# A graph network's tile loop: three stretches of first-layer units a tile instead of two, and two-tile groups at the end

## The chip, the cores and the metric

One core of one Trainium2 chip. The metric is the device time of one launch in microseconds; the time before is the median of three runs.

## The reference, cut to what matters

```python
# 6250 nodes, 200000 edges sorted by destination, 200 edge types, D = 128
# layer 0: attention over the edges of each node
e = leaky_relu(a_src[src] + a_dst[dst] + a_rel[etype], 0.01)
w = exp(e - segment_max(e, dst)[dst])
agg = segment_sum(w / segment_sum(w, dst)[dst] * x[src], dst)
x = layernorm(x + where(deg > 0, agg, x) + x @ loop_weight)
# then two layers of this, h = x at first:
msg = (rel_embed[etype] + h[src]) @ W_r
h = rrelu(segment_sum(msg, dst) * deg ** -0.5 + where(deg == 0, h @ W_el, h @ W_sl))
# and out = layernorm(x + h)
```

## The kernel before, in words

The nodes are cut into 50 tiles of 125. The kernel has three parts: a loop over the tiles (attention and everything that the two later layers need), the rest of the first message layer, and the second message layer.

**The tile loop.** For tile t, POOL gathers the rows of the tile's edges (33 indirect transfers, L605, issued a tile ahead into one of two buffers). VectorE adds the score terms (L1227, the first step of `weights`), works out the softmax's maxima in two exchanges with TensorE (L921 and L928), and ScalarE turns the result into 33 weighted one-hot matrices, which TensorE multiplies with the gathered rows (L938). Meanwhile VectorE prepares tile t+1: the wide comparisons on L1170, and in `prepare_edges` (L1197 on) two large tables of one-hots, one for the nodes, one for the 200 edge types; both are made on L1193, as are the smaller ones of the batches. TensorE multiplies the two tables in `types_in` (L836).

**The counts.** A tile's adjacency with all 50 source tiles is a matrix of counts, built in seven batches (`batch`: VectorE makes one-hots on L1193, TensorE multiplies them on L859, ScalarE copies them out, each batch needing the copy of the second one before). SyncE stores the matrix in HBM; `at_stored` counts the stores.

**Units and stretches.** The message of the first layer into a group of destination tiles is a sum over 52 units: two for the edge types and one for each of the 50 source tiles. A unit can be computed when the source tile has left the loop (`hs_ready`) and the counts of the whole group are stored. It is three matmuls (L872) with one column for each destination node of the group: 500 for a group of four tiles, 250 for the last one, of two. There are 12 groups of four and one of two.

A table made when the program is built (L84 to L94) gives each tile, from tile 6 on, up to two stretches: at most 12 consecutive units of one group each, the group with the most units ready first. A stretch (`stretch`) is loaded in pieces of four units into `held`, which has two places: a piece can be loaded (L518, `load_held`, on SyncE's queue) when the piece two before it is done (`held_done`). A stretch accumulates in PSUM bank 6, and VectorE adds it to the group's sum (`stretch_sum`, L1306) before the next stretch may begin (`st_read`).

The order on each engine is written out by hand. On TensorE, for a tile between the first and the last: the small products for the maxima; stretch 0, piece 0; the accumulation L938; `terms`; stretch 0, piece 1; batch 0; stretch 0, piece 2; batches 1 and 2; `types_in` of the next tile; batch 3; `types`; stretch 1, piece 0; batches 4 to 6; `x1_in` (a transposition); stretch 1, piece 1; `x1_node` (the node product, L898); stretch 1, piece 2. On VectorE: `weights`, `prepare_wide`, batches 0 and 1, `prepare_edges`, the sum of stretch 0, batch 2, `finalize`, batch 3, `normalise`, batches 4 to 6, `terms`; the sum of stretch 1 stands at the head of the next tile's `weights`, ahead of L1227. On SyncE: the lists of tile t+2, the loads of pieces 1 and 2 of stretch 0, the wide lists, `reshape_terms` (L491 to L496: a store of the score terms, a wait for it, and a load), the loads of stretch 1, and then `store_counts`.

**The rest of the first layer.** What the stretches left over (148 units) is loaded through a ring (`load_piece`) and multiplied group by group. VectorE finishes a group in two steps (`finish`, L1393 and L1396), and then each of its tiles gets a node product (L994, `node_m`), which ScalarE and VectorE turn into the second layer's weights; TensorE puts a group's node products between the units of the next. **The second layer** (L1037, L1039) runs over the 50 destination tiles.

## Time and profile before

| | |
|---|---|
| median of three runs | 2718.59 us (2717.42 to 2721.06) |
| the profiled execution | 2715.95 us, span 2714.0 us |
| TensorE busy | 2153.3 us, 79% of the span |
| VectorE busy | 1971.8 us, 73% |
| POOL busy | 1584.6 us, 58% |
| ScalarE busy | 1219.5 us, 45% |
| tile loop | up to 2157 us |
| rest of the first layer | 2157 to 2282 us |
| second layer | 2282 us to the end |

The profile comes from one execution. PE is TensorE, PEld its weight loads, DVE is VectorE, ACT ScalarE, POOL GpSimd, SP SyncE. In brackets stands how long the engine stood idle just before an instruction, and what ended that.

### The profile page before, as it was taken

Reading aid. Unit: us, or ns where it says so; the run is one execution under the profiler, and the core shown is the slowest. Engines: PE = TensorE matmul, PEld = TensorE weight load, DVE = VectorE, ACT = ScalarE, POOL = GpSimd, SP = SyncE. Lnnn points to the kernel's source line nnn. Section 1 sums busy time; section 2 is a strip of 40 time slices with the busy share of each in tenths; the row PEclk is TensorE's granted clock in tenths of the full one; section 3 lists DMA queues with packets and bytes.
Section 4 is the critical chain, followed back from the end, with each engine's and each line's share of the span. In section 5 each row is a group of like instructions: output and inputs, shape, how many; then the busy total and the mean of one; then the engine's idle time right before and its main releaser. Section 6 shows DMA issues by size and latency. Waiting matters only on the chain. (4 is left out here: it accounts for less than half of the span.)

```text
span 2714.0 us, 44262 instructions
## 1 busy us (share of the span) xinstructions
PE 2153.3 (79%) x15636; PEld 1612.5 (59%) x15636; DVE 1971.8 (73%) x4330; ACT 1219.5 (45%) x3215; POOL 1584.6 (58%) x1672
## 2 busy tenths in 40 slices
PE   1466676767677787786887878888888889999998
PEld 0355565655555555655565656556656536888887
DVE  6788888888888888878888888888778562333333
ACT  1265565565555555554555555655545441000000
POOL 6767777777777777777777777777777000000000
PEclk9888888888888888898988989989999999999999
DMA  8545555656555565655666667667666435666664
GB/s 226 173 127 158 174 157 161 195 156 190 173 184 174 177 193 166 210 181 180 215 186 198 217 183 217 200 198 234 197 211 209 144 108 186 213 213 212 214 214 154
DMA packets 265971, 507.43 MB, mean 187 GB/s; under 512 B 106240, under 2 KB 203832, under 8 KB 245921
## 3 DMA queue, kind: packets, MB, share of 16 engines
q1 hardware_dynamic: 197394, 383.10, 43.3%
q0 software_dynamic: 53600, 114.17, 16.3%
q10 hardware_dynamic: 14752, 7.26, 1.0%
q8 instruction: 128, 2.10, 0.3%
q14 instruction: 97, 0.79, 0.1%
HBM read 406.54 MB, written 97.84 MB: 186 GB/s over the span
## 5 line engine op out<-in xcount | busy, mean ns | idle before, releaser
L605 POOL DMA_INDIRECT arena<-rows,srcw x1617 | 1535.0, 949 | 510.4 <-issue 490.7
L1193 DVE TENSOR_TENSOR arena<-bank,idx 128x2000 bf16<-128x2000 bf16 (+3 forms) x700 | 562.1, 854 | 93.6 <-PE pair L859 87.8
L859 PE MATMUL pair<-arena 128*128 128x250 bf16 x2500 | 344.5, 286 | 283.1 <-DVE arena L1193 273.2
L627 ACT ACTIVATE arena<-pair 99x264 f32<-99x264 f32 (+2 forms) x410 | 282.3, 713 | 556.3 <-PE pair L859 420.1
L729 ACT ACTIVATE arena<-arena,wexp 128x125 f32<-128x125 bf16 x1650 | 483.3, 385 | 1.6
L872 PE MATMUL bank<-arena 125*128 125x500 bf16 (+1 forms) x1950 | 465.2, 387 | 12.2 <-DMA arena<-counts 11.7
L859 PEld LDWEIGHTS pair<-arena 128*128 128x128 bf16 x2500 | 243.5, 102 | 372.5 <-DVE arena L1193 308.3
L938 PE MATMUL bank<-arena 128*125 128x130 f32 x3300 | 448.8, 295 | 0.0
L938 PEld LDWEIGHTS bank<-arena 128*125 128x125 f32 x3300 | 417.2, 201 | 24.3
L1039 PE MATMUL pair<-arena 125*125 125x384 bf16 x2500 | 414.8, 326 | 0.0
L1039 PEld LDWEIGHTS pair<-arena 125*125 125x125 bf16 x2500 | 341.0, 136 | 66.1 <-issue 0.4
L1170 DVE TENSOR_TENSOR arena<-arena,bank 128x4224 bf16<-128x4224 int16 x150 | 344.2, 2350 | 1.7
L872 PEld LDWEIGHTS bank<-arena 125*128 125x128 bf16 x1950 | 189.0, 100 | 229.7 <-issue 67.4
L836 PE MATMUL pair<-arena 128*125 128x200 bf16 x1650 | 210.5, 305 | 10.1 <-DVE arena L1193 10.1
L836 PEld LDWEIGHTS pair<-arena 128*125 128x125 bf16 x1650 | 209.2, 181 | 12.9 <-issue 10.9
L1411 DVE SCALAR_TENSOR_TENSOR arena<-pair,norm,arena 125x128 f32<-125x128 f32 x50 | 17.5, 351 | 272.1 <-PE pair L1039 272.1
L776 ACT ACTIVATE rstd<-mv,epst 125x1 f32<-125x1 f32 x50 | 14.7, 294 | 407.5 <-DVEq L1433 407.5
L1193 DVE TENSOR_TENSOR arena<-bank,et 128x6600 bf16<-128x6600 bf16 x50 | 179.2, 3584 | 0.0
L661 ACT ACTIVATE arena<-pair 128x500 bf16<-128x500 f32 x150 | 95.8, 639 | 108.7 <-PE pair L859 105.3
L1193 DVE TENSOR_TENSOR arena<-bank,dl 128x4224 bf16<-128x4224 bf16 x50 | 117.9, 2358 | 1.7
L1306 DVE TENSOR_TENSOR arena<-bank,arena 128x500 f32<-128x500 f32 x80 | 54.4, 679 | 47.8 <-PE bank L872 44.9
L826 PE MATMUL pair<-arena,Zd 125*3 125x264 bf16 x800 | 62.0, 278 | 29.8 <-DVE arena L1170 17.7
(243 smaller groups left out, 2009.6 us busy)
## 6 DMA issues: line engine op xcount, KB each, us to landing
arena<-counts SPq DMA_DIRECT2D x104, 812.5 KB, 4.5
counts<-arena SPq DMA_DIRECT2D x50, 1562.5 KB
arena<-counts SPq DMA_DIRECT2D x112, 500.0 KB, 3.8
arena<-dst SPq DMA_DIRECT2D x50, 1056.0 KB
arena<-etype SPq DMA_DIRECT2D x50, 1056.0 KB
arena<-rows,srcw POOLq DMA_INDIRECT x1617
arena<-counts SPq DMA_DIRECT2D x11, 750.0 KB, 4.4
arena<-counts SPq DMA_DIRECT2D x23, 250.0 KB, 4.1
```

Source lines behind the costliest of these rows:

```text
L605: pool.indirect_dma_start(out=rows[:, q, c, :], out_offset=None, in_=rows0, in_offset=bass.IndirectOffsetOnAxis(ap=srcw[:, q, c:c + 1], ax ...
L627: act.activation(o, i, ACT.Copy).then_inc(s("ev"), 1)
L661: act.activation(AT[:, :, d0:d0 + 2 * G], two, ACT.Copy)
L729: r = act.activation(hot[:, c % HOTS, :], hotb[:, c, 0:TN], ACT.Copy, scale=wexp[:, c:c + 1])
L826: pe.matmul(o, Zd[0:TN, t % 2, 0:3], hotT[0:TN, cs], start=True, stop=False)
L836: r = pe.matmul(b_[0:TN, 0:R], hotb[:, c, 0:TN], toh[:, c, :], start=(c == 0), stop=(c == C - 1))
L859: r = pe.matmul(group_of(n, gi), ohl[:, sl, gi * GC + c, :], ohm[:, sl, gi * GC + c, :], start=(c == 0), stop=(c == GC - 1))
L872: r = pe.matmul(o, w, moving[0:n_], start=start and j == 0, stop=stop and j == 2)
L938: r = pe.matmul(sums[0:TN, 0:D + 2], hot[:, c % HOTS, :], rows[:, q, c, 0:D + 2], start=(c == 0), stop=(c == C - 1))
L1039: r = pe.matmul(o, part[0:TN, u - u0, :], hs1[0:TN, u - 2, :], start=False, stop=(u == HS - 1))
L1170: return v.tensor_tensor(out_.rearrange("p (j t) -> p j t", t=2), list_.rearrange("p (j t) -> p j t", t=2), two[:, None, :].broadcast_to(s ...
L1193: return v.tensor_tensor(hot_.rearrange("p c (j t) -> p c j t", t=2), iotap[:, 0:w].rearrange("p (j t) -> p j t", t=2)[:, None, :, :].broa ...
```

## The change

It does five things. The thirteen groups become fourteen: eleven of four tiles and three of two (`GSIZES`); a piece of a two-tile group holds eight units. From tile 30 on a tile has a third stretch, of at most 8 units of a four-tile group, and its pieces, like those of stretch 1, stand between the batches. The second stretch may take a group as soon as its last tile is a tile behind, the first one a tile later as before. On VectorE, `prepare_edges` is cut in two, and batch 2 stands between the halves; the sum of stretch 0 stands behind the second. On TensorE the first two units of stretch 0 are issued apart: one ahead of the products for the maxima, one between the two exchanges.

```diff
@@ -76,34 +76,42 @@
...
 GT = 4
-NGR = -(-NT // GT)
+GSIZES = (4,) * 11 + (2,) * 3
+GAT = [sum(GSIZES[:g_]) for g_ in range(len(GSIZES) + 1)]
+NGR = len(GSIZES)
+GROUP_OF = [g_ for g_ in range(NGR) for _ in range(GSIZES[g_])]
 HOTS = 26
 NU = 4
-SLEN = 3 * NU
+THIRD = 30
+SLENS = (3 * NU, 3 * NU, 2 * NU)
 STRETCH, DONE_U = {}, [0] * NGR
 for t_ in range(6, NT):
-    for k_ in range(2):
+    for k_ in range(3 if t_ >= THIRD else 2):
         best = None
         for g_ in range(NGR - 1):
-            n_ = min(SLEN, t_ + 1 + k_ - DONE_U[g_])
-            if GT * g_ + GT + 1 <= t_ and n_ >= 2 and STRETCH.get((t_, 0), (NGR,))[0] != g_ and (best is None or n_ > best[0]):
+            w_ = GSIZES[g_]
+            n_ = min(SLENS[k_] * GT // w_, t_ + (1, 1 if t_ >= THIRD else 2, 2)[k_] - DONE_U[g_])
+            if GAT[g_ + 1] + (k_ == 0) <= t_ and n_ * w_ >= 2 * GT and STRETCH.get((t_, k_ - 1), (NGR,))[0] != g_ \
+                    and (best is None or n_ * w_ > best[0] * GSIZES[best[1]]):
                 best = (n_, g_)
-        if best is not None:
-            n_, g_ = best
-            STRETCH[t_, k_] = (g_, DONE_U[g_], DONE_U[g_] + n_)
-            DONE_U[g_] += n_
+        if best is None:
+            break
+        n_, g_ = best
+        STRETCH[t_, k_] = (g_, DONE_U[g_], DONE_U[g_] + n_)
+        DONE_U[g_] += n_
 STRETCHES = list(STRETCH)
...
     g_, u_, e_ = STRETCH[key_]
-    for i_ in range(-(-(e_ - u_) // NU)):
+    nu_ = NU * GT // GSIZES[g_]
+    for i_ in range(-(-(e_ - u_) // nu_)):
         HELD_AT[key_ + (i_,)] = len(HELD)
-        HELD.append((key_, g_, u_ + i_ * NU, min(u_ + i_ * NU + NU, e_)))
+        HELD.append((key_, g_, u_ + i_ * nu_, min(u_ + i_ * nu_ + nu_, e_)))
     HELD_TO[key_] = len(HELD)
...
 def tiles_of(g):
-    return range(GT * g, min(GT * g + GT, NT))
+    return range(GAT[g], GAT[g + 1])
 
...
@@ -514,9 +522,10 @@
...
                     sp.wait_ge(s("held_done"), n - 1)
-                sp.wait_ge(s("at_stored"), 32 * GT * (g + 1))
-                sp.dma_start(held[:, n % 2, 0:GT * (u1 - u0) * TN].rearrange("p (t f) -> p t f", t=GT),
-                             counts[GT * g:GT * g + GT, :, u0 * TN:u1 * TN].rearrange("t p f -> p t f")).then_inc(s("held%d" % (n % 2)), 16)
+                w = GSIZES[g]
+                sp.wait_ge(s("at_stored"), 32 * GAT[g + 1])
+                sp.dma_start(held[:, n % 2, 0:w * (u1 - u0) * TN].rearrange("p (t f) -> p t f", t=w),
+                             counts[GAT[g]:GAT[g + 1], :, u0 * TN:u1 * TN].rearrange("t p f -> p t f")).then_inc(s("held%d" % (n % 2)), 16)
 
...
@@ -560,6 +569,8 @@
...
                 load_held(t, 1, 2)
+                load_held(t, 2, 0)
+                load_held(t, 2, 1)
                 load_held(t + 1, 0, 0)
...
@@ -872,21 +883,24 @@
...
 
-            def stretch(t, k, i):
+            def stretch(t, k, i, a=0, b=None):
                 if (t, k, i) not in HELD_AT:
...
                 m = STRETCHES.index(key)
-                if i == 0 and m >= 1:
+                v0, v1 = min(u0 + a, u1), u1 if b is None else min(u0 + b, u1)
+                if i == 0 and a == 0 and m >= 1:
                     pe.wait_ge(s("st_read"), m)
...
                 pe.wait_ge(s("held%d" % (n % 2)), 16 * (n // 2 + 1))
-                part = held[:, n % 2, 0:GT * (u1 - u0) * TN].rearrange("p (t u d) -> p t u d", t=GT, d=TN)
-                for u in range(u0, u1):
-                    r = unit(per_tile(bank[6][:, 0:GT * TN], GT), part[:, :, u - u0, :], u, u == STRETCH[key][1], u == STRETCH[key][2] - 1)
-                r.then_inc(s("held_done"), 1)
+                w = GSIZES[g]
+                part = held[:, n % 2, 0:w * (u1 - u0) * TN].rearrange("p (t u d) -> p t u d", t=w, d=TN)
+                for u in range(v0, v1):
+                    r = unit(per_tile(bank[6][:, 0:w * TN], w), part[:, :, u - u0, :], u, u == STRETCH[key][1], u == STRETCH[key][2] - 1)
+                if v0 < v1 == u1:
+                    r.then_inc(s("held_done"), 1)
 
...
@@ -917,6 +931,7 @@
...
                     self_in(t + 1)
+                stretch(t, 0, 0, 0, 1)
                 pe.wait_ge(s("th_ready"), t + 1)
...
@@ -924,10 +939,11 @@
...
                     own_turned(t - 1)
+                stretch(t, 0, 0, 1, 2)
                 pe.wait_ge(s("cf_ready"), t + 1)
...
                 pe.matmul(bank[0][:, 2 * P + 1:2 * P + 2], cfb[0:1, 1, :], ones[0:1, 0:1], start=True, stop=True).then_inc(s("cf_ps"), 1)
-                stretch(t, 0, 0)
+                stretch(t, 0, 0, 2)
                 if t >= 1:
...
@@ -977,21 +993,33 @@
...
                     stretch(t, 1, 0)
-                    for j in range(4, BT):
-                        batch(t, j)
+                    batch(t, 4)
+                    if (t, 2) in STRETCH:
+                        stretch(t, 1, 1)
+                    batch(t, 5)
+                    if (t, 2) in STRETCH:
+                        stretch(t, 1, 2)
+                    batch(t, 6)
                     x1_in(t)
-                    stretch(t, 1, 1)
+                    if (t, 2) in STRETCH:
+                        stretch(t, 2, 0)
+                    else:
+                        stretch(t, 1, 1)
                     x1_node(t)
-                    stretch(t, 1, 2)
+                    if (t, 2) in STRETCH:
+                        stretch(t, 2, 1)
+                    else:
+                        stretch(t, 1, 2)
 
...
@@ -1195,6 +1223,10 @@
...
             def prepare_edges(t):
+                edge_nodes(t)
+                edge_types(t)
+
+            def edge_nodes(t):
                 q = t % 2
...
@@ -1205,6 +1237,8 @@
...
                 paired(hotb, dl2, C)
+
+            def edge_types(t):
                 paired(toh, et2, C).then_inc(s("hot_ready"), 1)
...
@@ -1218,7 +1252,7 @@
...
                 if t >= 1:
-                    stretch_sum(t - 1, 1)
+                    stretch_sum(t - 1, 2 if (t - 1, 2) in STRETCH else 1)
                 v.wait_ge(s("dr_summed"), t + 1)
...
@@ -1370,17 +1405,20 @@
...
                         batch(t, j)
-                    if more:
-                        prepare_edges(t + 1)
+                    edge_nodes(t + 1)
+                    batch(t, 2)
+                    edge_types(t + 1)
                     stretch_sum(t, 0)
-                    batch(t, 2)
                     finalize(t)
...
                         batch(t, j)
+                    if (t, 2) in STRETCH:
+                        stretch_sum(t, 1)
                 if more:
                     terms(t + 1)
+            stretch_sum(NT - 1, 2)
             v.wait_ge(s("st_read"), len(STRETCHES))
```

What is left out replaces `GT * g` by `GAT[g]` and `GT` by the group's own width in `stretch_sum`, `finish` and `node_m`.

## Rows read from the trace of the kernel before

**Rows 1.** The page: a group of part 5, and an issue of part 6.

```profile
L605 POOL DMA_INDIRECT arena<-rows,srcw x1617 | 1535.0, 949 | 510.4 <-issue 490.7
...
arena<-counts SPq DMA_DIRECT2D x112, 500.0 KB, 3.8
```

**Rows 2.** Stretches of time: PE, PEld, DVE, ACT, POOL busy; PEclk, DMA share, GB/s.

```profile
1330.00:2120.00 790.00, 671.04 (x5066) 473.11 (x5066) 659.69 (x1367) 437.95 (x1144) 589.93 (x624) 0.93 0.66 202
...
2157.00:2240.00 83.00, 71.75 (x282) 33.95 (x281) 47.69 (x149) 36.19 (x132) 0.00 (x0) 1.00 0.38 116
```

**Rows 3.** Timeline, L1227 on DVE in tiles 26, 30, 49; the last gather on POOL.

```profile
1161.67 0.21 DVE L1227 TENSOR_TENSOR u<-arena,dr 128x33 f32<-128x33 f32 x1 [2.80 <-DMA arena<-rows,srcw]
...
1329.24 0.20 DVE L1227 TENSOR_TENSOR u<-arena,dr 128x33 f32<-128x33 f32 x1
...
2108.86 0.94 POOL L605 DMA_INDIRECT arena<-rows,srcw  x1 [0.30 <-issue]
...
2119.65 0.20 DVE L1227 TENSOR_TENSOR u<-arena,dr 128x33 f32<-128x33 f32 x1
```

**Rows 4.** Timeline of DVE in tile 46, 1992.5 to 2035 us.

```profile
1992.59 0.20 DVE L1227 TENSOR_TENSOR u<-arena,dr 128x33 f32<-128x33 f32 x1
...
2012.94 3.59 DVE L1193 TENSOR_TENSOR arena<-bank,et 128x6600 bf16<-128x6600 bf16 x1
...
2017.56 1.79 DVE L1193 TENSOR_TENSOR arena<-bank,idx 128x2000 bf16<-128x2000 bf16 x2
...
2021.23 1.79 DVE L1193 TENSOR_TENSOR arena<-bank,idx 128x2000 bf16<-128x2000 bf16 x2
...
2028.76 1.41 DVE L1193 TENSOR_TENSOR arena<-bank,idx 128x1500 bf16<-128x1500 bf16 x2 [2.33 <-PE pair L859]
...
2033.75 0.68 DVE L1306 TENSOR_TENSOR arena<-bank,arena 128x500 f32<-128x500 f32 x1 [3.25 <-PE bank L872]
...
2034.35 0.20 DVE L1227 TENSOR_TENSOR u<-arena,dr 128x33 f32<-128x33 f32 x1
```

**Rows 5.** Timeline of PE in tile 46, 1998 to 2036 us.

```profile
2019.40 1.04 PE L859 MATMUL pair<-arena 128*128 128x250 bf16 x8 [2.41 <-DVE arena L1193]
...
2020.28 2.99 PE L836 MATMUL pair<-arena 128*125 128x200 bf16 x33
...
2025.36 2.71 PE L872 MATMUL bank<-arena 125*128 125x500 bf16 x12 [1.11 <-DMA arena<-counts]
...
2030.23 0.82 PE L859 MATMUL pair<-arena 128*128 128x250 bf16 x6 [0.85 <-DVE arena L1193]
...
2035.12 0.38 PE L921 MATMUL bank<-ident,lf 128*1 128x128 f32 x2 [0.66 <-DVE lm_in L1230]
```

**Rows 6.** Timeline of SP in tile 46, 2004 to 2030 us.

```profile
2020.69 0.39 SPq L496 DMA_DIRECT2D drw<-edge_terms  x1
...
2021.18 0.98 SPq L518 DMA_DIRECT2D arena<-counts  x2
```

**Rows 7.** Timeline of PE in tile 34, 1519 to 1529 us.

```profile
1521.63 1.04 PE L859 MATMUL pair<-arena 128*128 128x250 bf16 x8 [2.47 <-DVE arena L1193]
...
1522.51 4.65 PE L836 MATMUL pair<-arena 128*125 128x200 bf16 x33
```

**Rows 8.** Timeline of DVE, L1396 of groups 0, 10, 11 and 12.

```profile
2160.38 0.68 DVE L1396 SCALAR_TENSOR_TENSOR arena<-arena 128x500 f32<-128x500 f32 x1
...
2234.53 0.68 DVE L1396 SCALAR_TENSOR_TENSOR arena<-arena 128x500 f32<-128x500 f32 x1
...
2262.59 0.68 DVE L1396 SCALAR_TENSOR_TENSOR arena<-arena 128x500 f32<-128x500 f32 x1
...
2282.55 0.42 DVE L1396 SCALAR_TENSOR_TENSOR arena<-arena 128x250 f32<-128x250 f32 x1
```

**Rows 9.** Timeline of PE after the loop, 2239 to 2284 us.

```profile
2240.53 21.31 PE L872 MATMUL bank<-arena 125*128 125x500 bf16 x99
...
2267.00 15.06 PE L872 MATMUL bank<-arena 125*128 125x250 bf16 x138
```

18 lines of the change are left out of this document (10 added, 8 removed).

## The prediction

> **What bounds the kernel now.** I read the grouped lines first, to find an engine that never rests in the tile loop. It is POOL: 1617 gathers of 0.949 us with 490.7 us of issue gaps between them and next to no waiting [rows 1]. One gather costs 1.25 us, so the 33 of a tile take 41.2 us, and no tile can be quicker than that. The stretches of time come next [rows 2]: between 1330 and 2120 us (tiles 30 to 48) TensorE is busy for 671 of 790 us and VectorE for 660, neither of them full. From 2157 us the loop is over and the rest of the first layer runs, and from 2282 us the second layer, which TensorE fills and the change does not touch.
>
> Then I followed one instruction through the tiles, the addition on L1227 that opens a tile's softmax; I call its time u. At 1161.67 us (tile 26) it still waits 2.80 us for the gather, so up to there POOL sets the pace. At 1329.24 (tile 30) and 2119.65 (tile 49) it waits for no gather any more, and the last gather was issued at 2108.86 [rows 3]. So 19 tiles took 790.4 us, 41.6 each, where POOL alone asks for 41.2, and at the end the loop is some 9 us behind the gathers. **From tile 30 on it is not POOL but the exchange between VectorE and TensorE that decides, by a small margin.** That is the place where the change adds work.
>
> Inside tile 46 (u = 1992.59, next u = 2034.35, period 41.76) VectorE has the nodes' table behind it and starts the types' table on L1193 at u+20.4, then the one-hots of batch 2 at u+25.0 and of batch 3 at u+28.6, ready at u+30.4 [rows 4]. TensorE waits 2.41 us ahead of batch 2, runs the types table in 2.99 us, and starts the first piece of the second stretch at u+32.8, after 1.11 us of waiting for its load [rows 5]. That load was issued only at u+28.6, because SyncE stood at the reshaped terms, whose last transfer it issues at u+28.1 [rows 6]. From u+32.8 everything on TensorE stands in the way of the next tile: 8 units of a stretch, three batches, a transposition. The sum on L1306 waits 3.25 us for the last unit, and the next u follows it at once [rows 4]. **A unit put ahead of batch 3 is free as long as it fills the hole; a unit put behind it is paid in full.**
>
> **The change, step by step.** One unit of a four-tile group is three matmuls of 500 columns; 99 of them take 21.31 us, 0.215 each, 0.644 us a unit. 138 matmuls of 250 columns take 15.06 us, 0.109 each [rows 9]. A unit of a two-tile group is thus 0.327 us and costs per tile what the wide one does. Below, n counts four-tile units and two narrow ones are one.
>
> (1) The tail after the loop. The plan leaves 148 units before (56 in groups 0 to 10, 40 in group 11, 52 narrow ones in group 12) and 105 after (45 in groups 0 to 10, 8 narrow ones in groups 11 and 12, 52 narrow ones in group 13). Groups 0 to 10 finish on L1396 from 2160.38 to 2234.53, ten steps of 7.4 us [rows 8], while TensorE is busy for 71.75 of 83 us [rows 2]: node products and units, partly overlapped. Eleven units fewer are worth between 0 and 7 us; I take 3. Group 11 then finishes at 2262.59 and group 12 at 2282.55, 28.1 and 20.0 us further [rows 8]. In their place come two short groups, each between half a step and a whole one (3.7 to 7.4; I take 5, as each has two nodes but the whole handshake), and the last group with two interleaved node products fewer, 18.7 us: 28.7 in place of 48.0. The tail gains 19.3 + 3 = **22 us, between 17 and 26**.
>
> (2) The loop takes on what the tail gives up: 188 tile-units, 47 n, or 30 us of TensorE. But it also moves units. Which, the file's own planning loop tells (the one that the diff rewrites), worked through for both versions. In tiles 30 to 48 the first stretch, which lies ahead of batch 3, falls from 199 n to 134. The second and third, which lie behind it, rise from 121 to 220, since a new group now enters the second stretch as soon as it is complete (12 n in tiles 32, 36, 40, 44, 46 and 48) and the third adds 3 to 8 n in each tile. So 99 n move into the part that is paid.
>
> (3) Price of a tile. Before: 32.8 us to the first piece of stretch 1, 0.644 n, and 3.85 us for batches 4 to 6, the transposition and the sum (tile 46: 32.8 + 5.15 + 3.85 = 41.8). Summed over 19 tiles with 121 n this is 774 us against the 790.4 measured. The 16 us between are mostly clock: in tile 34 the types table takes 4.65 us, where it takes 2.99 in tile 46, after the same wait of 2.4 us [rows 7, 5], and the granted clock of the stretch is 0.93 [rows 2]. After: the wait of 0.85 us ahead of batch 6 [rows 5] is filled in tiles whose second stretch has more than one piece, and one node product (0.65 us) moves ahead of the last piece where the third has two; I leave 3.85. With the table again at 32.8, for the queue that sets the load is the same, 19 x 36.65 + 220 x 0.644 = 838 us, **48 us more than before**. Ends: if the first piece starts at u+31.6, the end of batch 3 and the small products without the load's wait, 23 us less, so +25; if the clock stays as it is, 16 more, and if each tile with a second piece in the third stretch waits for held loads, 9 more, so +73.
>
> (4) Batch 2 between the tables. VectorE does the same work in another order: batch 2 is ready near u+22.5 but the types table only near u+26.2, and batch 3 where it was, near u+31 (half a microsecond later, as batch 2 now waits for batch 0's products). TensorE's hole of 2.41 us is cut into one of about 1 ahead of the table and one of 1.7 behind it. Gain: nothing by itself, since batch 3 is what counts; if the table falls into the slow clock again it no longer delays batch 3, and that is why (3) takes the full clock.
>
> (5) The first piece's units spread. They fill the waits of 0.66 us for L921 [rows 5] and the like one behind it. The accumulation that follows waits for ScalarE's weights, so I cost this at nothing (0 to 0.2 us a tile, 4 in all). It adds a risk: L921, with the whole softmax chain behind it, now stands behind a held load. Such a load takes 3.8 us to land [rows 1] and can be issued only when the piece two before it is done; where the third stretch ends in a piece of one or two units that is 1 to 2 us late. This is the 9 us in (3).
>
> (6) 19 more sums on L1306 at 0.68 us [rows 4] are 13 us of VectorE; it waits 5.6 us in a tile for TensorE, so they hide, and one more is in the period of a tile only through its wait. SyncE's two more loads a tile stand ahead of the counts' store, which waits for the next tile's weights anyway.
>
> Tiles 6 to 29 also change (58 to 111 n behind batch 3), but there POOL has the pace and VectorE waits for the gathers, 2.80 us in tile 26 [rows 3]; that wait takes up the 1.4 us a tile that 53 n make, and is their only cover (without it they cost 34 us); I add 1 us for tile 30 starting later and nothing for tile 49.
>
> Sum: 48 + 1 - 22 = +27. The profiled execution took 2715.95 us (span 2714.0), the median of the runs is 2718.6, 2.6 us above. I forecast **2744 us** as a median: 2716 + 27 is 2743, and I round the 2.6 against the part of (5) that may gain. A difference within 0.2%, 5.4 us, can't be told from none.
>
> One rule of the Trainium skill speaks against the narrow groups. The rows say 0.109 us for 250 columns and 0.215 for 500, so no loss [rows 9]. TensorE: Matmul & The Clock Gate, section Back-to-back issue gap, gives for streams of weight load and matmul 81 ns at 128 columns and 131 at 512; an estimate from that page, 97 ns at 250 and 130 at 500, would make each of the 288 narrow matmuls in the loop 32 ns dearer than its half of a wide one, 9 us more. The trace does not agree, and the sum leaves it out.
>
> **The rivals.** A, faster: the third stretch falls into holes. If the loop keeps within POOL's pace, u of tile 49 can't come before the last gather has landed, about 2112 us, up to 8 us earlier than now, and the tail's 22 us come on top: 2718.6 - 22 and down to -30, so **2694**. For it speaks that TensorE stands idle for 119 of the 790 us [rows 2] and only 30 us are added; against it that these holes lie ahead of batch 3, where the plan takes units away. It decides if the third piece's start is below about u+30 in most tiles.
>
> B, the cost only cancels the gain: the first piece starts at u+31.6 and half the light tiles hide their third stretch, +22 in the loop: **2718**, no difference.
>
> C, slower still: the clock. The row shows half speed for the table after a wait of 2.4 us, in most tiles. If the two smaller holes pull it down as the one did, now in front of 12 units that are paid, the 16 us stay and the late loads of (5) come on top: **2768**. The same page's section on the clock gate says that the array falls to 1.2 GHz after idleness and comes back with sustained work; by that rule the denser tail of a tile should run at 2.4 GHz, which is my main case, and rows 7 agree with its first half.
>
> **How the numbers follow.** Main case 0.50 (own range 2724 to 2762), A 0.25, B 0.10, C 0.15. Faster 0.25, same 0.10, slower 0.65. The range takes half of A and most of C: 2695 to 2768.
>
> **What would show it.** In the profile after: L1227 from tile 30 to 49 some 838 us apart instead of 790; periods near 41 in tiles with 7 n behind batch 3 and near 47 in tiles 44, 46 and 48; no wait for gathers there; the last wait of L1306 or of L872 for a load in those tiles; L836 at 2.99 us or no longer followed by a late batch 3; group 13's finish about 103 us behind the loop's end in place of 125. I am wrong if the 19 tiles take under 800 us, which would mean that units behind batch 3 are not paid, or if the tail gains under 15.

## The result, and the profile after

The changed kernel takes **2781.05 us** (median, 2777.82 to 2784.44), the kernel before 2719.82 us beside it on the same chip (2717.42 to 2723.16): a ratio of 1.0225, interval 1.0212 to 1.0238. So it is slower by 61 us, where 27 were forecast; 2781 lies above the range, whose upper end was 2768. The profiled execution has a span of 2781.4 us against 2714.0, 67.4 us more. In twelve of the runs below the kernel before itself took 4448 to 4451 us, with stretches of some 20 us in which no engine works, so these runs stand apart at the end and nothing is read from them.

The page of the changed kernel, its costliest groups and the DMA issues. L616 is L605 of before, L883 is L872, L847 is L836, L870 is L859:

```profile
L616 POOL DMA_INDIRECT arena<-rows,srcw x1617 | 1536.5, 950 | 566.6 <-issue 487.4
...
L883 PE MATMUL bank<-arena 125*128 125x500 bf16 (+1 forms) x2100 | 456.1, 360 | 41.8 <-DMA arena<-counts 36.1
...
L847 PE MATMUL pair<-arena 128*125 128x200 bf16 x1650 | 230.7, 323 | 117.1 <-DVE arena L1221 107.6
...
arena<-counts SPq DMA_DIRECT2D x118, 500.0 KB, 5.2
```

Against [rows 1] a gather costs the same, but POOL now rests for 56 us more, and a held load of 500 KB lands after 5.2 us, not 3.8. TensorE waits 36.1 us for held loads.

The timeline of VectorE in the changed kernel, the addition that opens a tile (L1261, L1227 of before) in tiles 16, 17, 30 and 49, and POOL's last gather:

```profile
752.39 0.21 DVE L1261 TENSOR_TENSOR u<-arena,dr 128x33 f32<-128x33 f32 x1 [5.63 <-DMA arena<-rows,srcw]
801.10 0.20 DVE L1261 TENSOR_TENSOR u<-arena,dr 128x33 f32<-128x33 f32 x1
1349.48 0.20 DVE L1261 TENSOR_TENSOR u<-arena,dr 128x33 f32<-128x33 f32 x1
2204.75 0.20 DVE L1261 TENSOR_TENSOR u<-arena,dr 128x33 f32<-128x33 f32 x1
...
2168.07 0.95 POOL L616 DMA_INDIRECT arena<-rows,srcw  x1 [0.30 <-issue]
```

Against [rows 3]: tile 30 opens 20.2 us later, tile 49 85.1 us later, so tiles 30 to 48 took 855.3 us in place of 790.4. The finishes after the loop, L1434 (L1396 of before), of groups 0, 10, 11, 12 and 13:

```profile
2251.04 0.68 DVE L1434 SCALAR_TENSOR_TENSOR arena<-arena 128x500 f32<-128x500 f32 x1
...
2321.20 0.68 DVE L1434 SCALAR_TENSOR_TENSOR arena<-arena 128x500 f32<-128x500 f32 x1
...
2327.31 0.42 DVE L1434 SCALAR_TENSOR_TENSOR arena<-arena 128x250 f32<-128x250 f32 x1
...
2331.60 0.42 DVE L1434 SCALAR_TENSOR_TENSOR arena<-arena 128x250 f32<-128x250 f32 x1
...
2350.01 0.42 DVE L1434 SCALAR_TENSOR_TENSOR arena<-arena 128x250 f32<-128x250 f32 x1
```

Ten steps take 70.2 us (before 74.2), the last groups 6.1 + 4.3 + 18.4 = 28.8 us (before 28.1 + 20.0) [rows 8]. From u of tile 49 to the first finish it is 46.3 us, where it was 40.7.

**The four stretches add up.** Tiles 0 to 29 lose 20.2 us, tiles 30 to 48 lose 64.9, tile 49 loses 5.6, the tail gains 23.3: 67.4, the whole difference of the spans. The forecast had +1, +48, 0 and -22.

Inside a late tile, TensorE in tile 44 of the changed kernel (u = 1962.52, period 49.84, 17 n behind batch 3):

```profile
1964.48 0.80 PE L883 MATMUL bank<-arena 125*128 125x500 bf16 x3 [2.49 <-DMA arena<-counts]
...
1965.21 0.38 PE L936 MATMUL bank<-ident,lf 128*1 128x128 f32 x2
...
1970.35 0.19 PE L860 MATMUL bank<-onesb,arena 128*125 128x1 bf16 x1 [1.23 <-issue]
...
1990.20 4.65 PE L847 MATMUL pair<-arena 128*125 128x200 bf16 x33 [1.84 <-DVE arena L1221]
...
1997.72 1.44 PE L883 MATMUL bank<-arena,relW 128*128 128x500 bf16 x6 [1.68 <-DMA arena<-counts]
```

and VectorE there (L1269 reads the transposed row, L1341 is the sum of a stretch):

```profile
1965.84 0.41 DVE L1269 TENSOR_TENSOR_SCAN XY<-full,bank 1x128 f32<-1x128 f32 x1 [2.06 <-PE bank L937]
...
2006.98 0.68 DVE L1341 TENSOR_TENSOR arena<-bank,arena 128x500 f32<-128x500 f32 x1 [4.44 <-PE bank L883]
2011.76 0.68 DVE L1341 TENSOR_TENSOR arena<-bank,arena 128x500 f32<-128x500 f32 x1 [3.78 <-PE bank L883]
```

The first unit, spread ahead of the transposition L936, waits 2.49 us for its load, and VectorE waits 2.06 us for the transposition behind it. In tile 46 of before nothing stood there but 0.66 us for VectorE [rows 5]. The stretch sums wait 8.2 us in the tile, the last with the next u right behind it: units behind batch 3 are paid.

SyncE's queue in tiles 43 and 44 of the changed kernel (L527 issues the held loads; the first row is the last reshaped term, after which they go out):

```profile
1947.53 0.39 SPq L504 DMA_DIRECT2D drw<-edge_terms  x1
1948.01 0.43 SPq L527 DMA_DIRECT2D arena<-counts  x1
1950.77 0.27 SPq L516 DMA_DIRECT2D dense_input<-arena  x1
1951.14 9.85 SPq L527 DMA_DIRECT2D arena<-counts  x3
1970.32 0.34 SPq L510 DMA_DIRECT2D counts<-arena  x1
```

Three held loads go out one by one from 1951.1 to 1961.0, each as TensorE gives a buffer back; the last is the next tile's first piece. It leaves 1.5 us ahead of u and lands 3.5 us later.

Grouped lines of TensorE by form, 1350 to 2205 us, tiles 30 to 48 of the changed kernel (busy, mean ns | idle before, by what):

```profile
L883 PE MATMUL bank<-arena 125*128 125x500 bf16 x930 | 220.7, 378 | 19.5 <-DMA arena<-counts 16.6 <-DVE arena L1341 2.7
...
L847 PE MATMUL pair<-arena 128*125 128x200 bf16 x627 | 84.7, 316 | 38.4 <-DVE arena L1221 31.3 <-ACT arena L638 7.1
...
L883 PE MATMUL bank<-arena 125*128 125x250 bf16 x204 | 26.0, 285 | 1.7 <-DMA arena<-counts 1.7
...
L944 PE MATMUL bank<-ones,cfb 1*128 1x1 f32 x38 | 7.4, 261 | 2.9 <-DVE cfb L1272 2.9
...
L860 PE MATMUL bank<-onesb,arena 128*125 128x1 bf16 x19 | 3.6, 192 | 25.2 <-issue 22.3 <-ACT arena L740 2.8
...
L883 PE MATMUL bank<-arena,relW 128*128 128x500 bf16 x12 | 3.2, 374 | 5.6 <-DMA arena<-counts 5.6
```

And the same of the kernel before, 1330 to 2120 us:

```profile
L872 PE MATMUL bank<-arena 125*128 125x500 bf16 x936 | 228.5, 393 | 3.2 <-DMA arena<-counts 3.2
...
L836 PE MATMUL pair<-arena 128*125 128x200 bf16 x627 | 80.9, 307 | 0.0
...
L928 PE MATMUL bank<-ones,cfb 1*128 1x1 f32 x38 | 7.2, 256 | 16.9 <-DVE cfb L1238 16.9
```

TensorE lost 14 us of waiting at L928's place, but got 22.3 us ahead of L860, the accumulation that needs ScalarE's weights, and the wait for held loads rose from 3.2 us to 22 in the two rows of wide units alone (16.6 and 5.6). The types table did not get quicker: 84.7 us of TensorE for 19 tables, where 80.9 were before.

**Where a late tile got longer.** Every period can be cut in three, as step (3) of the prediction does: the start of the second stretch's first piece on TensorE, counted from u; 0.644 us a unit; and the rest. In tiles 30 to 48 the forecast had 32.8 us for the start and 3.85 for the rest. The timeline has, in the mean, 33.66 and 3.84 before, and 33.47 and 4.09 in the changed kernel: 12.7 and 4.6 us above the forecast over 19 tiles.

### The profile page after: what moved, and what is told of

It reads as the page before. It is cut to its first block and busy times, and to the rows that moved or that the text cites. A ratio compares the mean times of both kernels' runs of the same rounds, so it can differ in the third digit from the quotient of the medians.

```text
span 2781.4 us, 44709 instructions
## 1 busy us (share of the span) xinstructions
PE 2182.9 (78%) x15792; PEld 1653.5 (59%) x15792; DVE 1978.5 (71%) x4351; ACT 1219.8 (44%) x3215; POOL 1587.3 (57%) x1672
## 5 line engine op out<-in xcount | busy, mean ns | idle before, releaser
L616 POOL DMA_INDIRECT arena<-rows,srcw x1617 | 1536.5, 950 | 566.6 <-issue 487.4
L883 PE MATMUL bank<-arena 125*128 125x500 bf16 (+1 forms) x2100 | 456.1, 360 | 41.8 <-DMA arena<-counts 36.1
L954 PE MATMUL bank<-arena 128*125 128x130 f32 x3300 | 483.3, 308 | 0.0
L954 PEld LDWEIGHTS bank<-arena 128*125 128x125 f32 x3300 | 447.4, 212 | 28.4
L870 PE MATMUL pair<-arena 128*128 128x250 bf16 x2500 | 322.7, 275 | 158.2 <-DVE arena L1221 142.5
L870 PEld LDWEIGHTS pair<-arena 128*128 128x128 bf16 x2500 | 235.6, 99 | 240.8 <-DVE arena L1221 186.0
L883 PEld LDWEIGHTS bank<-arena 125*128 125x128 bf16 x2100 | 198.0, 98 | 232.6 <-issue 66.3
L847 PE MATMUL pair<-arena 128*125 128x200 bf16 x1650 | 230.7, 323 | 117.1 <-DVE arena L1221 107.6
L847 PEld LDWEIGHTS pair<-arena 128*125 128x125 bf16 x1650 | 221.5, 192 | 130.7 <-issue 108.4
L1341 DVE TENSOR_TENSOR arena<-bank,arena 128x500 f32<-128x500 f32 (+1 forms) x99 | 66.1, 668 | 141.1 <-PE bank L883 139.8
```

The costliest lines, as they stand in the source:

```text
L616: pool.indirect_dma_start(out=rows[:, q, c, :], out_offset=None, in_=rows0, in_offset=bass.IndirectOffsetOnAxis(ap=srcw[:, q, c:c + 1], ax ...
L847: r = pe.matmul(b_[0:TN, 0:R], hotb[:, c, 0:TN], toh[:, c, :], start=(c == 0), stop=(c == C - 1))
L870: r = pe.matmul(group_of(n, gi), ohl[:, sl, gi * GC + c, :], ohm[:, sl, gi * GC + c, :], start=(c == 0), stop=(c == GC - 1))
L883: r = pe.matmul(o, w, moving[0:n_], start=start and j == 0, stop=stop and j == 2)
L954: r = pe.matmul(sums[0:TN, 0:D + 2], hot[:, c % HOTS, :], rows[:, q, c, 0:D + 2], start=(c == 0), stop=(c == C - 1))
L1341: v.tensor_tensor(a, per_tile(bank[6][:, 0:w * TN], w), a, ALU.add).then_inc(s("st_read"), 1)
```

## The experiments

The disputed parts are four: the third stretch, the rule by which a new group enters the plan, the spread first piece, and batch 2 between the tables. The six runs beside a kernel before of 2719 to 2722 us come first. The other twelve stand at the end of this section with what they were expected to show.

**Run a4c: the old entry rule.** The third stretch stays, but a new group waits one tile, as before.

```diff
-            if GAT[g_ + 1] + (k_ == 0) <= t_ and n_ * w_ >= 2 * GT and ...
+            if GAT[g_ + 1] + 1 <= t_ and n_ * w_ >= 2 * GT and ...
```

> Once more, alone on its chip: the changed kernel with the old rule for when a group may enter a stretch, so that a new group's first 12 units go to the first stretch: 54 instead of 111 four-tile units behind batch 3 in tiles 6 to 29, 188 instead of 220 in tiles 30 to 48. If the place of a unit decides: the 20 us of delay at tile 30 go, and 20 more behind it: 2741. If only the number of units counts, no difference: 2781.

Measured: 2750.04 us, ratio 1.0108 (1.0091 to 1.0125), 31 us less than the changed kernel and 9 above what was expected. Its tiles 30 and 49 on VectorE:

```profile
1329.59 0.21 DVE L1261 TENSOR_TENSOR u<-arena,dr 128x33 f32<-128x33 f32 x1 [2.87 <-DMA arena<-rows,srcw]
...
2162.68 0.20 DVE L1261 TENSOR_TENSOR u<-arena,dr 128x33 f32<-128x33 f32 x1
```

The delay up to tile 30 is gone, to 0.3 us, and u waits for the gather again. The rule is what cost the 20 us there, and another 22 us in tiles 30 to 48 (833.1 us with 188 n behind batch 3, against 855.3 with 220). The run does not tell the burst from the amount: it has 54 n behind batch 3 in tiles 6 to 29 instead of 111, and puts them in no tile more than 4.

**Run a1c: the first piece whole.** The changed kernel, but all units of the first piece behind the second exchange, as before.

```diff
-                stretch(t, 0, 0, 0, 1)
...
-                stretch(t, 0, 0, 1, 2)
...
-                stretch(t, 0, 0, 2)
+                stretch(t, 0, 0)
```

> Once more, alone on its chip: the changed kernel with the first piece of stretch 0 whole again, behind the second exchange for the maxima. If a unit ahead of L936 makes the softmax chain wait for its held load (1.3 to 2.6 us in tiles 33, 43, 44, 45, 47, 48 and 49 of the changed kernel's trace, 14 us in all), 2767 us. If the spread units only fill holes, no difference: 2781. If they gained a hole's 0.65 us in the other tiles, 2790.

Measured: 2758.6 us, ratio 1.0148 (1.0131 to 1.0165), 22 us less than the changed kernel and 8 below what was expected of it. Grouped lines of TensorE by form, 1339 to 2183 us (L935 and L943 are L936 and L944 of the changed kernel):

```profile
L883 PE MATMUL bank<-arena 125*128 125x500 bf16 x930 | 228.0, 395 | 7.9 <-DMA arena<-counts 7.5
...
L935 PE MATMUL bank<-ident,lf 128*1 128x128 f32 x38 | 7.2, 271 | 17.9 <-DVE lm_in L1262 17.9
...
L860 PE MATMUL bank<-onesb,arena 128*125 128x1 bf16 x19 | 3.5, 184 | 1.8 <-issue 1.8
```

The load's wait falls by 9.1 us in the wide units (16.6 to 7.5) and the 22.3 us ahead of L860 are gone, while TensorE waits 17.9 us for the first exchange. So the spread had only moved TensorE's wait from the exchange to the weights, and put a load on the path of the softmax. Tiles 30 to 48 took 844.4 us (1338.63 to 2182.98), 10.9 less, and 10.8 came off before tile 30. The 10.9 lie where the first unit had waited for its load: tiles 33, 43, 44, 45, 47 and 48 are 11.3 us shorter together, the other thirteen 0.4 longer. The first piece of the second stretch now starts at u+32.87 in the mean, 0.60 earlier, and no unit waits ahead of the first exchange any more.

**Run d1b: no third stretch, old entry rule.** Groups of two, the tables' order and the spread stay.

```diff
-THIRD = 30
+THIRD = NT
...
-            if GAT[g_ + 1] + (k_ == 0) <= t_ and n_ * w_ >= 2 * GT and ...
+            if GAT[g_ + 1] + 1 <= t_ and n_ * w_ >= 2 * GT and ...
```

> Again, since the kernel before took 4448 us on the chip of the last run: the changed kernel without the third stretch and with the old entry rule; two-tile groups, spread first piece and the tables' order kept. Against the kernel with the old rule (2750) it has 128 four-tile units behind batch 3 in tiles 30 to 48 instead of 188, and 33 more left for the tail: 39 us less in the loop by 0.64 us a unit, no late first pieces, 10 to 20 us more in the tail: 2700 to 2715. If the third stretch filled holes, 2760 to 2770. If the tail's gain from two-tile groups is what my sum said, it ends below the kernel before.

Measured: 2720.28 us, ratio 1.0008 (0.9998 to 1.0018): no difference from before, and 5 us above what was expected. Against a4c this prices the third stretch: 60 n fewer behind batch 3, tiles 30 to 48 in 800.8 us in place of 833.1 (0.54 us a unit), and 30 us by the medians. The 0.54 is too low as the price of a unit, for these tiles had become quick enough to meet the gathers again: u waits 12.8 us for them in tiles 31 to 41. Its finishes of groups 10 to 13:

```profile
2251.94 0.68 DVE L1434 SCALAR_TENSOR_TENSOR arena<-arena 128x500 f32<-128x500 f32 x1
...
2258.06 0.42 DVE L1434 SCALAR_TENSOR_TENSOR arena<-arena 128x250 f32<-128x250 f32 x1
...
2268.69 0.42 DVE L1434 SCALAR_TENSOR_TENSOR arena<-arena 128x250 f32<-128x250 f32 x1
...
2287.09 0.42 DVE L1434 SCALAR_TENSOR_TENSOR arena<-arena 128x250 f32<-128x250 f32 x1
```

Groups 11 to 13 take 35.2 us instead of 48 for the last two of before, but the ten steps ahead of them 81.1 (from 2170.87) instead of 74.2. The plan leaves 72 wide units in groups 0 to 10 and 32 narrow ones in groups 11 and 12, where before left 56 and 40 wide ones in group 11. What the small groups gain in the tail is mostly spent on the older ones.

**Run e1: the same with the first piece whole.** The edits of a1c and d1b together.

> The changed kernel without its third stretch, with the entry rule of before and with the first piece whole again behind the second exchange; groups of two tiles and the tables' order stay. The kernel with these but with a spread first piece took 2720.3 us (before 2719.0). Theory: the spread costs in every tile in which GpSimd's list does not set the pace, because a held load that lands late then stops TensorE ahead of the exchanges: 22 us were found beside the third stretch (11 of them by tile 30); here only tiles 42 to 48 are free of GpSimd's pace, 7 tiles by 0.6 to 1.2 us: 2713 to 2717 us, tile 48 and 47 long as before (48.6 and 44.6 us). Rival: the spread costs only beside a third stretch or beside twelve units of a new group behind batch 3: 2720, no change. Rival: it pays where it stands alone: 2722 to 2725.

Measured: 2717.33 us, ratio 0.9993 (0.9984 to 1.0002), against 1.0008 with the spread. Tiles 30 to 48 took 796.1 us (1332.10 to 2128.21), 4.7 less than in d1b, of which 3.5 in tile 47 (45.2 us, was 48.6), which was expected to stay. The time is at the upper end of what the theory gave, and the two intervals overlap by a little, so I call it likely, not shown, that the spread costs some 3 us even alone. It is the best version found, and can't be told from the kernel before.

**Run b2b: batch 2 between the tables, alone**, in the kernel before.

```diff
-                    if more:
-                        prepare_edges(t + 1)
-                    stretch_sum(t, 0)
-                    batch(t, 2)
+                    edge_nodes(t + 1)
+                    batch(t, 2)
+                    edge_types(t + 1)
+                    stretch_sum(t, 0)
```

> The kernel before with batch 2 alone moved between the next tile's node tables and its type tables; groups, two stretches and the whole first piece stay. Theory (from the changed kernel's first five tiles, which took 36.5 to 37.5 us in place of 38.6 to 40.1): about 1.9 us a tile are saved where GpSimd's list does not set the pace: tiles 1 to 5 (then taken back by GpSimd's pace up to tile 41), and tiles 42 to 48; 2705 to 2715 us. Rival: the table order gains nothing anywhere but in tiles 1 to 5, where nothing stands behind batch 3: 2718 to 2721. Rival: batch 3's start moves later with the stretch sum and the order costs a little: 2722 to 2728.

Measured: 2719.47 us, ratio 0.9998 (0.9988 to 1.0007). The rival holds: no gain. Grouped lines of TensorE, 1330 to 2126 us:

```profile
L872 PE MATMUL bank<-arena 125*128 125x500 bf16 x936 | 236.4, 403 | 12.7 <-DMA arena<-counts 12.7
L859 PE MATMUL pair<-arena 128*128 128x250 bf16 x950 | 119.5, 271 | 48.8 <-DVE arena L1193 48.6
L836 PE MATMUL pair<-arena 128*125 128x200 bf16 x627 | 66.2, 271 | 29.5 <-ACT arena L627 16.7 <-DVE arena L1193 12.8
```

The order does for the types table what I expected: 66.2 us for 19 tables in place of 80.9, 14 of them at 3.02 us, where before only two ran at 2.99. The table now starts behind a wait of its own (29.5 us in all) and the units wait 12.7 us for loads, where they waited 3.2. Still the first piece of the second stretch starts at u+33.02 in the mean, where it was u+33.66: 12.0 us earlier over the 19 tiles. And yet these tiles took 795.6 us (1330.04 to 2125.67), 5.2 more than before. The trace shows two things that took the gain.

The first is POOL's pace. Tiles 31 to 36 now open with 9.0 us of waiting for gathers, tile 31 most of all, where before no tile behind 26 did:

```profile
1371.39 0.21 DVE L1233 TENSOR_TENSOR u<-arena,dr 128x33 f32<-128x33 f32 x1 [3.27 <-DMA arena<-rows,srcw]
```

The second is the clock. It left the table and fell on units that are paid: the first 12 matmuls of the second stretch take 5.16, 4.24, 4.24 and 4.38 us in tiles 37, 38, 41 and 46, with a granted clock of 0.50 to 0.61 over them, and 2.71 us before. Tile 37 of b2b, TensorE and the stretch of time (columns as in [rows 2], the granted clock is 0.50), and the same piece before:

```profile
1650.61 1.04 PE L859 MATMUL pair<-arena 128*128 128x250 bf16 x8 [1.80 <-DVE arena L1193]
...
1652.78 5.16 PE L872 MATMUL bank<-arena 125*128 125x500 bf16 x12 [1.02 <-DMA arena<-counts]
```

```profile
1652.70:1658.00 5.30, 5.22 (x14) 1.98 (x15) 1.13 (x2) 0.33 (x3) 4.07 (x5) 0.50 0.30 70
```

```profile
1650.61 2.71 PE L872 MATMUL bank<-arena 125*128 125x500 bf16 x12
```

Before, these matmuls took 0.23 or 0.24 us each in all 19 tiles. The four tiles are 7.6 us longer behind the piece's start. So of the 12.0 us gained, 9.0 went into waits for gathers and 7.6 into the lower clock: 4.6 more than was gained, of the 5.2 us lost. This is one execution, 3.8 us above b2b's median; how often the clock falls on these pieces is not known. That the earlier start is worth nothing is therefore not shown: the kernel before had only some 8 us to gain here before it met the gathers (19 times 41.2 us is 783, against 790.4). Tiles 1 to 5, which have no stretches, did get 1.6 us shorter in the mean (37.4 to 37.8 us, where they took 38.6 to 40.1), and POOL's pace took that back.

**Run c2b: another way to use the hole ahead of batch 3.** Groups of two with the old rule, the old order and a whole first piece, plus a fourth piece of the first stretch ahead of batch 2, and the second stretch's first load issued a step earlier. The sum of stretch 0 moves behind batch 3. The edit on TensorE:

```diff
-SLENS = (3 * NU, 3 * NU, 2 * NU)
+SLENS = (4 * NU, 3 * NU, 2 * NU)
...
-                    for j in range(1, 3):
-                        batch(t, j)
+                    batch(t, 1)
+                    stretch(t, 0, 3)
+                    batch(t, 2)
```

> The kernel with two-tile groups alone, a fourth piece of the first stretch ahead of batch 2, and the load of the second stretch's first piece issued ahead of SyncE's wait for the stored terms, once more: in the eight runs above the kernel before took 4432 to 4457 us, with stretches of 20 us in which no engine worked, so their differences say nothing of this case. If the kernel before takes 2720 again: 2675 to 2685 where units ahead of batch 3 are free and the load holds the second stretch; 2690 where only the first holds; 2705 to 2715 where a unit is paid wherever it stands. If the kernel before takes 4450 again, the 20 us stretches belong to the chip of these runs.

Measured: 2778.4 us, ratio 1.0217 (1.02 to 1.0234), a clear miss. The fourth piece on TensorE in tile 30 (u = 1336.22), and SyncE's queue there (L494 loads two wide lists of 1056 KB each, L499 stores the terms, L530 is a held load):

```profile
1368.82 3.91 PE L888 MATMUL bank<-arena 125*128 125x500 bf16 x9 [6.38 <-DMA arena<-counts]
```

```profile
1355.69 0.36 SPq L494 DMA_DIRECT2D arena<-dst  x1
1356.15 0.38 SPq L494 DMA_DIRECT2D arena<-etype  x1
1356.58 1.44 SPq L499 DMA_DIRECT2D edge_terms<-arena  x4
1358.18 3.81 SPq L530 DMA_DIRECT2D arena<-counts  x2
```

The load was issued at 1358.2 and TensorE could go on at 1368.8: 10.6 us for a held load behind 2.1 MB on the same queue, where such a load lands in 3.8 [rows 1]. In tiles 30 to 48 TensorE waits 60.7 us for held loads, where it waited 3.2 before. A tile with a fourth piece took about 47 us (1336.22 to the next u at 1383.49). That the lists are what delays the load is read from the order of the queue and not tested; a version that moves them behind it was not tried.

**The twelve other runs.** Each is given with its ratio to a kernel before of 4448 to 4451 us. First those whose kernel was seen again above. a1 and a1b are a1c's kernel, 4428.89 and 4434.86 us (0.9959, 0.9964):

> The changed kernel with the first piece of stretch 0 whole again, behind the second exchange for the maxima. If a unit ahead of L936 makes the softmax chain wait for its held load (1.3 to 2.6 us in tiles 33, 43, 44, 45, 47, 48 and 49 of the changed kernel's trace, 14 us in all), 2767 us. If the spread units only fill holes, no difference: 2781. If they gained what a hole is worth in the other tiles (0.65 us), 2790.

> Again, on a chip where the kernel before takes 2720 us: the changed kernel with the first piece of stretch 0 whole again, behind the second exchange for the maxima. If a unit ahead of L936 makes the softmax chain wait for its held load (1.3 to 2.6 us in tiles 33, 43, 44, 45, 47, 48 and 49, 14 us in all), 2767 us. If the spread units only fill holes, no difference: 2781. If they gained a hole's 0.65 us in the other tiles, 2790.

a4 and a4b are a4c's, 4437.22 and 4440.77 us (0.9974, 0.9979):

> The changed kernel with the old rule for when a group may enter a stretch, so that a new group's first 12 units go to the first stretch, ahead of batch 3: 54 instead of 111 units behind it in tiles 6 to 29, 188 instead of 220 in tiles 30 to 48. If the place of a unit decides: the 20 us of delay at tile 30 go, and 20 more behind it: 2741. If only the number of units counts, no difference: 2781.

> Again, on a chip where the kernel before takes 2720 us: the changed kernel with the old rule for when a group may enter a stretch, so that a new group's first 12 units go to the first stretch: 54 instead of 111 four-tile units behind batch 3 in tiles 6 to 29, 188 instead of 220 in tiles 30 to 48. If the place of a unit decides: the 20 us of delay at tile 30 go, and 20 more behind it: 2741. If only the number of units counts, no difference: 2781.

b2 is b2b's, 4400.18 us (0.9897):

> The kernel before with batch 2 between VectorE's two tables alone. If batch 3 sets the tile's end and comes at the same time, 2720, within 4. If the types' table at half clock, 4.65 instead of 2.99 us in 15 tiles, was on the path and is now off it, up to 16 us less: 2704. If the later types' table delays, 2730.

c2 is c2b's, 4388.72 us (0.9867):

> The same with the load of the second stretch's first piece issued ahead of SyncE's wait for the stored terms. If that load is what holds the piece (1.1 us in tile 46 of the kernel before), up to 1 us less a tile in tiles 30 to 48: 2675 to 2685. If batch 3 holds it anyway, as with the kernel above.

d1 is d1b's, 4413.05 us (0.9922):

> The changed kernel without the third stretch and with the old entry rule; two-tile groups, spread first piece and the tables' order kept. Against the kernel with the old rule (2750) it has 128 four-tile units behind batch 3 in tiles 30 to 48 instead of 188, and 33 more left for the tail: 39 us less in the loop by 0.64 us a unit, no late first pieces, 10 to 20 us more in the tail: 2700 to 2715. If the third stretch filled holes, 2760 to 2770. If the tail's gain from two-tile groups is what my sum said, it ends below the kernel before.

Then four kernels that were seen only so; what they would do beside a kernel before of 2719 us is open. a2, the changed kernel with both tables together ahead of batch 2, 4476.84 us (1.0066):

```diff
-                    batch(t, 2)
                     edge_types(t + 1)
                     stretch_sum(t, 0)
+                    batch(t, 2)
```

> The changed kernel with VectorE's two tables together again and batch 2 behind them and the sum. If the paid time begins behind batch 3, and batch 3 comes at the same time either way, no difference: 2781, within 5. If the reordering is what costs (the types' product now waits 2.55 us in most tiles), 2740 to 2760. If it holds up the clock, 2795.

a3, the changed kernel with `THIRD = NT`, the new entry rule kept, 4419.17 us (0.9941):

> The changed kernel without the third stretch: 160 four-tile units behind batch 3 in tiles 30 to 48 instead of 220, and some 31 more left for the tail. If each such unit is paid at 0.64 us in the loop: 39 us less there, the late first pieces go too (10), and 12 to 20 us more in the tail: 2746 to 2756. If the third stretch is not what costs, the tail alone shows: 2797.

b1, groups of two alone (d1b with a whole piece and a2's order), 4450.77 us and, as b1b, 4455.09 (1.0016, 1.0010):

> The kernel before with the groups of two tiles at the end alone (two stretches, old entry rule, old order). 7 more four-tile units behind batch 3 in tiles 30 to 48 (4.5 us), and the tail shorter by 17 to 22 us: 2703, within 5. If the short groups' handshakes eat the gain, or narrow matmuls cost more than half of wide ones, 2715 to 2720.

> Again, on a chip where the kernel before takes 2720 us: the kernel before with the groups of two tiles at the end alone (two stretches, old entry rule, old order). 7 more four-tile units behind batch 3 in tiles 30 to 48 (4.5 us), and the tail shorter by 17 to 22 us: 2703, within 5. If the short groups' handshakes eat the gain, or narrow matmuls cost more than half of wide ones, 2715 to 2720.

c1, c2b's kernel without the earlier load, 4387.90 us (0.9874):

> The kernel with two-tile groups alone, and a fourth piece in the first stretch, put ahead of batch 2, where TensorE waits 2.4 us; the sum of that stretch moves behind batch 3. 219.5 four-tile units ahead of batch 3 instead of 199, 116 behind it instead of 128, and 15 fewer left for the tail. If a unit ahead of batch 3 is free: 8 us less in the loop and up to 10 in the tail against the groups alone: 2690, within 6. If it is paid wherever it stands, 2705 to 2715.

How little these ratios carry over, one kernel shows: c2 was 1.3% faster than the kernel before, and the same kernel as c2b 2.2% slower.

**Five of the first six runs and the changed kernel side by side**, differences to the kernel before by its stretches, in us; worked out from the rows of u and of the last finish, the sum being the difference of the spans:

| kernel | n behind batch 3, tiles 30 to 48 | up to tile 30 | tiles 30 to 48 | from tile 49 on | sum |
|---|---|---|---|---|---|
| b2b, order alone | 121 | +0.8 | +5.2 | +1.3 | +7.3 |
| e1, groups and order | 128 | +2.9 | +5.7 | -5.7 | +2.9 |
| d1b, and the spread | 128 | +0.4 | +10.4 | -6.3 | +4.5 |
| a4c, and the third stretch | 188 | +0.4 | +42.7 | -13.6 | +29.4 |
| after, and the entry rule | 220 | +20.2 | +64.9 | -17.7 | +67.4 |
| a1c, after with a whole piece | 220 | +9.4 | +53.9 | -20.7 | +42.6 |

By its median b2b takes as long as before, though its profiled span is 7.3 us longer: terms of 5 us in one line of the table are within what single executions differ by, those of 20 and more are not.

## Why the prediction was wrong

The sign and the main place were right: units moved behind batch 3 are paid. Of the 40 us that the forecast was short, 19 lie before tile 30, 17 in tiles 30 to 48, 6 in tile 49, and the tail gave 1 back. Two steps failed, the cover of tiles 6 to 29 and the cost of the spread. Taken out of the change alone, the entry rule gives back 38.0 us of the span (67.4 to 29.4) and the spread 24.8 (67.4 to 42.6). Ahead of tile 30 the two overlap: the spread costs 10.8 us there with the bursts and nothing without them (a4c, +0.4). With a whole first piece the forecast would have been 15.6 us short.

**The cover of tiles 6 to 29: the first step that failed.** I wrote that the wait for gathers "takes up the 1.4 us a tile that 53 n make" and added 1 us. An average can't be hidden so. The plan puts 12 n into the one tile in which a group enters (12, 16, 20, 24 and 28, and 10 n in tile 8; before no tile had more than 4). Tile 16 opened with 5.63 us of waiting for its gathers and took 48.7 us, tiles 20 and 24 took 51.9 and 51.6 where POOL asks for 41.2. What a burst exceeds the slack by is lost; of the tiles behind it those of 37.8 to 39.5 us win back 2 or 3 us each, and the others take 40.3 to 41.7. a1c keeps the bursts and is 9.4 us late at tile 30; the other 10.8 come with the spread. a4c, which takes the bursts away, has all of it back. My own sentence named the cover's worth, 34 us; I should have priced the largest tile, not the mean.

**Step (5), the spread: the second that failed.** "I cost this at nothing (0 to 0.2 us a tile, 4 in all)", with 9 us of risk: it cost 22 us by the medians beside the rest of the change. The gain I named is no gain, because the accumulation waits for the weights anyway; this I had written, and the 22.3 us ahead of L860 show it. The risk was undersized: in tiles 43, 44, 45 and 48 the held load held back the first exchange for 2.3 to 2.6 us, in 33 and 47 for 1.3 and 1.7, together 12.8 us, and a1c's tiles 30 to 48 are shorter by 10.9. The other 10.8 us lie almost wholly in the burst tiles 16, 20 and 24 (3.4, 5.1 and 3.5), where the second stretch's first load is awaited 2.8, 2.7 and 2.4 us, and 0, 1.8 and 1.4 us with a whole piece. Behind that wait six of the paid matmuls take 427 to 452 ns each, and 240 in a1c; the granted clock over them is 0.50 or 0.51, so the lower clock fell on them too. What delays the load there I haven't traced further.

**Step (3), the price of a tile, held.** 838 us forecast, 855.3 measured, of which the spread has 10.9: with a whole piece it is 844.4, 6.4 above the sum. The start of the second stretch's first piece, forecast at u+32.8, is u+32.87 in a1c; the rest, forecast at 3.85 us, is 4.11. The 16 us of before lie whole in the late start (u+33.66 instead of 32.8), and in a1c they are gone, as the sum had it. But the full clock that the step took for the table did not come back: a1c's tables are as slow as before (82.2 us against 80.9), and it is the order of step (4) that keeps them out of the way. So the 64.9 us are 47.6 of price, 10.9 of the spread and 6.4 that stay unexplained. The slopes between runs are poor checks of the 0.644 us a unit: 0.54 from d1b to a4c (32.3 us for 60 n) and 0.53 from e1 to a1c (48.3 us for 92 n) come from d1b and e1, where u waits 12.8 and 5.0 us for gathers in tiles 31 to 41, and the 0.69 from a4c to the changed kernel (22.2 us for 32 n) has late loads in it.

**Step (4), the order, held as far as the traces show.** "Gain: nothing by itself" is b2b's result, though not for the reason given: the start came 12.0 us earlier, and the gathers and the lower clock took that. That a slow table "no longer delays batch 3" is what a1c shows: in tile 48 the table takes 5.73 us, from u+25.8, and the first piece starts at u+32.5; in tile 34 of before it takes 4.65 us, from u+28.1, and the piece starts at u+33.6. No run among the first six takes the order alone out of the changed kernel.

**Step (1), the tail.** 22 us forecast, 23.3 measured: the three small groups took 28.8 us, forecast 28.7, and the ten steps gained 4.0, forecast 3. But "nothing for tile 49" was wrong: it also has a third stretch, and from its u to the first finish it lost 5.6 us. It has 4 n more behind batch 3, 2.6 us at 0.644, and its first spread unit waits 2.32 us for its load.

**Step (6)** held. The sum in the middle of tile 44 waits 4.44 us for TensorE before it runs, so VectorE had room for one more; only the last one is in the period, as before.

**The rivals.** C came nearest in time, 2768, and half its mechanism was there: late loads stood on top and the clock stayed at 0.93 in tiles 30 to 48. But the 16 us did not stay (a1c), the lower clock fell on paid units only in tile 45 there (12 matmuls in 4.38 us) and in the burst tiles 16, 20 and 24, and the bursts themselves were lacking. A fell: in no late tile did the third stretch fall into a hole. What it saw, TensorE idle for 119 of 790 us, is idle time ahead of batch 3, and c2b shows that units put there must have their load in time. The rule about narrow matmuls did not bite: in the loop of the changed kernel 204 narrow ones took 26.0 us, 0.127 each, and 930 wide ones 220.7, 0.119 for a half: 9 ns dearer, and in a1c 23.5 and 228.0 us, 7 ns cheaper. The estimate from TensorE: Matmul & The Clock Gate of the Trainium skill (Back-to-back issue gap) was 32 ns dearer. The measurement decides.

**What stays open**: whether the bursts would be harmless if spread over three tiles; how much of the rule's 22 us in late tiles is units and how much is bursts; what the new order alone is worth in tiles that the gathers do not pace; what groups of two alone are worth, since b1's kernel is not among the first six runs.

## What to carry to other kernels

A slack that repeats in every tile covers only what comes in every tile: price the fullest tile of a plan, not its mean, against a pace set by another engine whose work can't run ahead. Do not put work that depends on a transfer ahead of an exchange on the critical path to fill a hole, unless the work behind it, here the accumulation that needs the weights, would really start earlier. When an edit shortens one piece of work and the time stays, look whether a wait for another engine took its place before calling the piece free: b2b started its paid part 12.0 us earlier and waited 9.0 us more for gathers. And moving work from a tail into a loop pays only by what it takes out of the tail: the third stretch cost 32.3 us in the loop and returned 7.4.

## What the hardware showed that I had not expected

The lower clock can move from one piece of work to the next. b2b took 14 of 19 tables out of it, and in four of these tiles it fell on the units behind: 353 to 430 ns a matmul in place of 226, with a granted clock of 0.50 in tile 37, after waits of 1.80 and 1.02 us. A held load's time to land differed between the kernels: 3.8 us as a median before, 5.2 in the changed kernel, and 10.6 in tile 30 of c2b, where two lists of 1056 KB went out on SyncE's queue just before it. No run isolates the queue as the cause.
